# First splits of the first quad and of wo moved into the stage before, A1 loaded in the fold, and ScalarE's order in attention

## The reference

```python
x = x + attn(cond(x, ids1))      # cond: x W1^T + b1 + 2 (x A1[ids1]) B1[ids1]
x = x + ffn(cond2(x, ids2))      # cond2 and ffn: a linear layer each, and experts of rank 16 and 64, top 2

def attn(x):                     # 32 query heads, 8 key/value heads of 128
    q, k, v = x @ wq, x @ wk, x @ wv
    q, k = rope(q), rope(k)
    scores = q k^T * 128 ** -0.5, causal, within a sequence
    return softmax(scores) v @ wo
```

## Time and profile before

| | |
|---|---|
| median of 3 runs | 2829.83 us (2829.41 to 2833.12) |
| profiled execution | 2826.46 us, its span 2824.5 us |
| mean granted clock of TensorE | 0.986 |
| TensorE busy | 2701.7 us, 96% of the span |
| GpSimd busy | 1198.7 us, 42% |
| VectorE busy | 1344.0 us, 48% |
| ScalarE busy | 854.5 us, 30% |
| chain that ended last | TensorE 85%, GpSimd 6%, ScalarE 3%, DMA 2% |

### The profile page before, as it was taken

One profiled execution on the slowest core, in us unless ns is written; L12 is line 12 of the kernel. 1 busy time (PEld: TensorE's weight loads), 2 busy tenths in 40 slices (PEclk: granted clock), 3 DMA queues, 4 the chain that ended last, 5 costly groups with the idle time before them and its releaser, 6 DMA issues.

```text
span 2824.5 us, 37498 instructions
## 1 busy us (share of the span) xinstructions
PE 2701.7 (96%) x14520; PEld 2174.1 (77%) x14520; DVE 1344.0 (48%) x2011; ACT 854.5 (30%) x2089; POOL 1198.7 (42%) x790
## 2 busy tenths in 40 slices
PE   8979899999998999999998989999999899999999
PEld 7857677777776788887877767777777678888877
DVE  2124667777775111124533557777777511112452
ACT  2222244444443312221212224444444331121110
POOL 0025665655665245510304476566555434441020
PEclk9999999999999999999999989999999999999999
DMA  6853122222225333111543312222222433311322
GB/s 217 243 145 119 45 68 73 70 75 68 71 62 189 126 113 105 51 39 54 145 124 100 109 45 76 75 74 63 67 75 72 168 127 112 105 53 38 84 86 70
DMA packets 311984, 268.47 MB, mean 95 GB/s; under 512 B 68218, under 2 KB 283386, under 8 KB 311810
## 3 DMA queue, kind: packets, MB, share of 16 engines
q1 hardware_dynamic: 250210, 210.50, 24.6%
q10 hardware_dynamic: 61600, 55.58, 6.0%
HBM read 201.88 MB, written 64.16 MB: 94 GB/s over the span
## 4 chain that ended last, share of the span: by engine, by line
PE 85%; POOL 6%; ACT 3%; DMA 2%; issue 2%; SPq 1%; DVE 1%; ACTq 0%; POOLq 0%
PE prod L658 25%; PE prod L660 24%; PE prod L659 24%; PE turned L901 3%; PE turned L851 2%; POOL s_lo L1465 2%; POOL o_lo L1499 1%; ACT probs L1227 1%; ACT s_hi L1213 1%; PE turned L652 1%; PE turned L884 1%; PE prod L1086 1%; POOL w_sum L1489 1%; PE prod L766 1%; POOL w_lo L1430 1%
## 5 line engine op out<-in xcount | busy, mean ns | idle before, releaser
L1430 POOL TENSOR_TENSOR w_lo<-raw,w_hi 128x1024 fp32r<-128x1024 f32 x96 | 239.2, 2493 | 850.0 <-ACT w_hi L1146 728.0
L658 PE MATMUL prod<-o_hi,w_hi 128*128 128x512 f32 x1024 | 405.4, 396 | 22.9 <-POOL o_lo L1499 19.2
L659 PE MATMUL prod<-o_lo,w_hi 128*128 128x512 f32 x1024 | 400.8, 391 | 0.0
L660 PE MATMUL prod<-o_hi,w_lo 128*128 128x512 f32 x1024 | 400.4, 391 | 0.0
L1784 DVE TENSOR_TENSOR x<-prod,x 128x512 f32<-128x512 f32 x128 | 88.5, 692 | 603.3 <-PE prod L660 603.3
L1465 POOL TENSOR_TENSOR s_lo<-w_sum,s_hi 128x512 fp32r<-128x512 f32 x192 | 253.0, 1318 | 155.7 <-ACT s_hi L1213 155.7
L658 PE MATMUL prod<-t_hi,s_hi 128*128 128x512 f32 x768 | 312.2, 407 | 3.9 <-POOL s_lo L1465 3.9
L1146 ACT CAST w_hi<-raw 128x1024 fp32r<-128x1024 f32 x128 | 134.1, 1048 | 599.7 <-PE prod L660 428.0
L660 PE MATMUL prod<-t_hi,s_lo 128*128 128x512 f32 x768 | 300.5, 391 | 0.0
L659 PE MATMUL prod<-t_lo,s_hi 128*128 128x512 f32 x768 | 299.8, 390 | 0.0
L658 PE MATMUL prod<-b_hi,s_hi 128*128 128x512 f32 x576 | 239.9, 417 | 15.7 <-POOL s_lo L1465 15.7
(11 more groups left out here) (168 smaller groups left out, 5063.5 us busy)
## 6 DMA issues: line engine op xcount, KB each, us to landing
raw_pair<-in_wq SPq DMA_DIRECT2D x64, 512.0 KB, 4.7
o_scratch<-o_out ACTq DMA_DIRECT2D x64, 512.0 KB, 2.9
raw<-in_wo SPq DMA_DIRECT2D x64, 512.0 KB, 4.0
o_raw<-o_scratch SPq DMA_DIRECT2D x64, 512.0 KB, 7.2
raw<-t_scratch SPq DMA_DIRECT2D x50, 512.0 KB, 3.6
t_scratch<-x ACTq DMA_DIRECT2D x17, 512.0 KB, 4.2
x_raw<-in_x SPq DMA_DIRECT2D x16, 512.0 KB, 5.9
xt_scratch<-x_sum SPq DMA_DIRECT2D x16, 512.0 KB, 3.2
```

Source lines behind the costliest of these rows:

```text
L658: pe.matmul(dst, wh, xh, start=start, stop=False)
L659: pe.matmul(dst, wh, xl, start=False, stop=False)
L660: return pe.matmul(dst, wl, xh, start=False, stop=stop)
L1430: pool.tensor_tensor(WL[i % 2][:], RAW[i % 2][:], WH[i % 2][:].bitcast(F32), ALU.subtract).then_inc(w_lo, 1)
```

## The change

1. `load_a1(0)` moves from the start of stage 1 into the fold loop, ahead of W2's tile 6, into a buffer of its own; `load_a1(1)` moves behind the loads of half 1's first two W1 tiles. ScalarE casts x's blocks 4 to 7 ahead of `AH`, VectorE makes their low parts ahead of `AL`. The cast of W1's tile 2 now stands ahead of the first `c_hi`; for half 1 the first two tiles' casts move within the end of half 0.
2. `load_pair` works in two halves (rows 0 to 511 and 512 to 1023), each with its semaphore. The first half of the next quad is requested after the fourth sum, the second after the sixth low part as before; for the first quad the halves wait for the last two W1 tiles. A k/v pair has now four DMAs instead of two. ScalarE casts the first quad's first two parts ahead of `b22`'s last activation.
3. In attention `turn_p` of the second score block moves from product 0 to product 1 of `QD_KV`, and ScalarE's `p_out` of it likewise, behind the casts `s_high(n + 1, 0)` and `s_high(n + 1, 1)`.
4. ScalarE casts wo's first two tiles at products 2 and 3 of the last quad and the first eight chunks at products 5 and 6. GpSimd makes both tiles' low parts, then chunks 0 to 11; chunks 12 to 15 are VectorE's (`o_lo_d`). The masks of the last group's third and fourth score block stand one product earlier on VectorE, and ScalarE's `exps` of the third.

The diff, cut to its core, in the order SP, TensorE, ScalarE, GpSimd, VectorE (`sp`, `pe`, `act`, `pool`, `dve` in the code):

```diff
-        AW = sb("lora_a_raw", [P, TT * D], offset=88 * KB)
+        AWS = [sb(f"lora_a_raw{hf}", [P, TT * D], offset=o * KB) for hf, o in enumerate((188, 88))]
...
+        def pair_count(n):
+            gg, qd = divmod(n, QUADS)
+            return 16 * (4 * gg + 2 + qd)
...
+        def o_lo_at(hf, kb, i):
+            return (hf * OKB + kb) * 16 - 4 * (hf + (kb > 0)) + i + 1
...
                 if 4 <= i < 8:
                     load_x(0, i - 4)
+                if i == 6:
+                    sp.wait_ge(const_in, 16 * 5)
+                    sp.wait_ge(fold_taken, 4)
+                    load_a1(0)
...
-                if g == 0 and qd == 0:
-                    sp.wait_ge(w_lo, pool_no(hf, T_WO - 1) + 1)
-                else:
-                    sp.wait_ge(s_lo, 7 * (n - 1) + 6)
+                for h in range(2):
+                    ks = slice(4 * h, 4 * h + 4)
+                    if g == 0 and qd == 0:
+                        sp.wait_ge(w_lo, pool_no(hf, T_WO - 2 + h) + 1)
+                    elif h == 0:
+                        sp.wait_ge(s_sum, 4 * (n - 1) + 4)
+                    else:
+                        sp.wait_ge(s_lo, 7 * (n - 1) + 6)
...
-                    sp.wait_ge(tw_turned, TW_N)
-                    load_a1(0)
                     load_x(0, TB - 1)
...
-                        if s == KC - 2:
-                            sp.wait_ge(taken, q_base + Q_O + 4 * 4 + 4)
-                            load_a1(hf + 1)
                 if hf + 1 < HALVES:
                     load_w1(hf + 1, 0)
                     load_w1(hf + 1, 1)
+                    sp.wait_ge(taken, q_base + Q_O + 4 * 4 + 4)
+                    load_a1(hf + 1)
...
-                                if at_ == (QD_KV, 0):
+                                if at_ == (QD_KV, 1):
                                     turn_p(gg - 1, 0, 1)
-                                if at_ == (QD_KV, 1):
                                     score(gg - 1, 1, 0)
...
-                                if j == 0:
-                                    pe.wait_ge(o_lo, (hf * OKB + kb) * 16 + t * KC + k + 1)
+                                if j == 0 and kb == 0 and t == 1 and k >= 4:
+                                    pe.wait_ge(o_lo_d, 4 * hf + k - 3)
+                                elif j == 0:
+                                    pe.wait_ge(o_lo, o_lo_at(hf, kb, t * KC + k))
...
+                for b in range(4, TB):
+                    x_hi(hf, b)
                 act.wait_ge(a_in, 16 * TT * SPT * (hf + 1))
...
-                act.copy(AH[:], AW[:]).then_inc(a_hi, 1)
-                for b in range(4, TB):
-                    x_hi(hf, b)
+                act.copy(AH[:], AWS[hf][:]).then_inc(a_hi, 1)
...
-                for n in range(KC):
+                tile_hi(hf, 2, QN["h0"])
+                c_hi(0)
+                for n in range(1, KC):
                     c_hi(n)
                     tile_hi(hf, n + 2, QN[f"c{n}.0"])
...
+                    if j == 3:
+                        s_high(pair_no(hf, 0, 0), 0)
+                        s_high(pair_no(hf, 0, 0), 1)
...
-                for i in (0, 1, 2, 4, 3, 5, 6):
+                for i in (2, 4, 3, 5, 6):
                     s_high(n0, i)
...
-                                if at_ == (QD_KV, 0):
+                                if at_ == (QD_KV, 1):
                                     p_out(4 * (gg - 1) + 1)
...
+                            if not more:
+                                if i == 2:
+                                    act.wait_ge(qprod, q_done(last, 1))
+                                    tile_hi(hf, T_WO)
+                                if i == 3:
+                                    act.wait_ge(qprod, q_done(last, 3))
+                                    tile_hi(hf, T_WO + 1)
+                                if i in (5, 6):
+                                    for c in range(4 * (i - 5), 4 * (i - 5) + 4):
+                                        o_high(0, c)
...
                 tile_lo(hf, T_WO)
-                for i in range(KC):
-                    o_low(0, i)
                 tile_lo(hf, T_WO + 1)
-                for i in range(KC, 2 * KC):
+                for i in range(KC + 4):
                     o_low(0, i)
...
-                dve.wait_ge(a_hi, hf + 1)
-                dve.tensor_tensor(AL[:], AW[:], AH[:].bitcast(F32), ALU.subtract).then_inc(a_lo, 1)
                 for b in range(4, TB):
                     x_lo(hf, b)
+                dve.wait_ge(a_hi, hf + 1)
+                dve.tensor_tensor(AL[:], AWS[hf][:], AH[:].bitcast(F32), ALU.subtract).then_inc(a_lo, 1)
...
+                for c in range(4, KC):
+                    dve.wait_ge(o_hi, hf * OKB * 16 + KC + c + 1)
+                    dve.tensor_tensor(chunk_of(o_lows(0), c, 1), chunk_of(o_lows(0, OWP), c, 1),
+                                      OH[0][:, c * TOK + NT:(c + 1) * TOK].bitcast(F32), ALU.subtract
+                                      ).then_inc(o_lo_d, 1)
...
+                            if kb == 0 and j == 0 and t == 0:
+                                mask(last_v + 2)
                             if kb == 0 and j == 0 and t == 1:
-                                mask(last_v + 2)
+                                mask(last_v + 3)
                             if kb == 0 and j == 1 and t == 0:
-                                mask(last_v + 3)
                                 normalise(last_v + 2)
```

More of the change, by code:

```diff
@@ L1416, in _ @@
                 if hf + 1 < HALVES:
-                    for i in range(2):
-                        act.wait_ge(raw_in[i], raw_count(hf + 1, i))
-                        act.wait_ge(prod, q_base + Q_O + 4 * (KC - 2 + i) + 2)
-                        act.copy(WH[i][:], RAW[i][:]).then_inc(w_hi, 1)
+                    tile_hi(hf + 1, 1, Q_O + 4 * (KC - 1) + 1 - Q_N)
                 store(KC - 1)
@@ L1471, in _ @@
                         pool.wait_ge(s_lo, 7 * n)
-                    pool.wait_ge(pair_in, 32 * (n + 1))
+                    for h in range(2):
+                        pool.wait_ge(pair_in[h], pair_count(n))
                     if n == pair_no(hf, 0, 0):
```

102 lines of the change are left out of this document (48 added, 54 removed).

## The result

The changed kernel takes 2788.07 us (median, 2785.69 to 2790.83), the kernel before beside it 2830.9: a ratio of 0.9848, 95% interval 0.9831 to 0.9865, 42.8 us faster. The prediction was 2785 us. The profiled execution has a span of 2783.7 us against 2824.5, so 40.8 less; the forecast for it was 44.4 less.

The account below looks back on a forecast made before the run. TensorE, busy 2701.7 of 2824.5 us, was taken to bound the kernel. Terms +9.5 -6.6 -2.9 -21.0 -23.4 = -44.4 take the median from 2829.83 to 2785 us, range 2773 to 2801.

Parts of the forecast that it names:

- Part 1: Fold: A1's half 0 loads on SP ahead of W2's tile 6 delay its products, +9.5 us, ends 8.5 and 12.
- Part 2: Start of half 0: xt_lo wait and c's tile wait go, a new LoRA wait of 4.7 comes; together -6.6 us.
- Part 3: Start of half 1: w_lo waits shrink or go, a new AL wait of 4.7 comes; -2.9 us, ends -9.3 and +2.6.
- Part 4: First quad, both halves: earlier casts and split pair loads shorten GpSimd's chain; -10.5 us each half, -21.0 in all.
- One sign: First quad: the profile after would show the s_lo waits down by over half.
- Part 5: Start of wo, both halves: o_lo starts earlier and VectorE takes four chunks; -11.7 us each half, -23.4 in all.
- Rival (e): Start of wo: o_hi's data or casts hold o_lo to 897.12, only VectorE's four gain; +11.6, 2797 us, chance 0.04.
- Part 6: Steady groups: the 1.35 wait hangs on a chain whose order the diff leaves; 0 us, one end -25.0.
- (a): Steady groups: one more VectorE and GpSimd collision in each of 14 groups, +11.9, 2797.3 us; chance 0.10.
- (b): Steady groups: four ops of each group collide with GpSimd, +66, 2851 us, slower than before; chance 0.03.
- (d): Steady groups: the steady waits go too through GpSimd's earlier start, -25.0, 2760.4 us; chance 0.05.

Follow-up runs that it names:

- the first two experiments on A1: Changed kernel with A1's half 0 loads moved: first, eight behind the fold, eight behind x's blocks 4 to 6, 2776.95 us; second, all ahead of x's block 7, 2776.29 us.
- the third experiment on A1: Changed kernel with A1's half 0 loads in SP's free time, and AH and AL ahead of x's blocks 4 to 7 in both halves: 2766.69 us.
- the last experiment on wo: Changed kernel with ScalarE's casts of wo's first two tiles and first eight chunks behind the last quad's work: 2807.58 us.
- the two swaps: Changed kernel with third block's normalise ahead of fourth's mask on VectorE, 2813.49 us; adding third block's p_out ahead of fourth's exponentials on ScalarE, 2762.35 us.
- the experiment with turn_p and p_out: Changed kernel with turn_p and p_out of the second score block back at product 0 of the k/v quad: 2791.36 us.

## Why the prediction was right, point by point

**Right in sign, size and place.** Every term has the sign that was forecast, and the sum, -44.4, is 3.8 from the profiled -40.6. Two errors are larger than 1 us.

**Part 1 was mis-sized**: +13.0 for +9.5, above its upper end of 12 (its lower end, without the clock, should read 8.7 by its own sum and not 8.5). The wait itself is 9.75 for 8.7, but that it came so near is luck, since the step named there is not the one that TensorE waits for. I had it wait for w_lo, behind a cast and a subtraction; it waits for raw, which the small products of the tile read as it is (L722). The split runs beside them:

```profile
117.99 1.23 DVE L1568 TENSOR_TENSOR w_lo<-raw,w_hi 128x1024 fp32r<-128x1024 f32 x1 [24.50 <-ACT w_hi L1119]
```

```profile
120.43 0.77 PE L672 MATMUL prod<-x_hi,w_hi 128*128 128x512 f32 x1
```

So the 2.4 us of cast, subtraction and hand-offs fall out of the sum. In their place the wait begins 1.7 us ahead of 109.00, where the small products stand, and SP's first A1 issue came at 94.32 and not at 92.4; why SP began 1.9 later is open. The larger miss in the size is the clock: I charged 0.8, and it was 10.2 us at 0.50, 2.9 lost. That the loss is SP's order alone is shown by the first two experiments on A1, that the early load buys nothing by the second of them. The load price, 4.0 by the row, was 4.3 here (issue at 112.58, landed at 116.89). The estimate of 3.2 by the Trainium skill's page DMA: Bandwidth & Descriptors, section Anatomy of one DMA — SWDGE (gpsimd) path, would have been further off.

**Part 2** was -5.7 for -6.6; the lora_a_lo wait is 4.63 for 4.7, w_lo's wait is gone. That wait and two of part 3 belong to a line that the earlier trace rows leaves out, the second of the full list before (8.1 in 3 after):

```profile
PE prod L658 <- POOL w_lo L1430: 19.4, 6, 4.6
```

**Part 3** was -2.9 for -2.9, with the same 4.63. But both parts took A1's place behind x's casts as the price of the gain, and the third experiment on A1 shows that it is none: with the load in SP's free time, AH and AL fit in ahead.

**Part 4** was -11.3 and -11.0 for -10.5 each. The casts ahead of stage 1's end and the split loads are both needed; the loads are worth somewhat more than the 2.8 and 1.0 that I gave them, through the half clock behind v_tok. One sign was missed: the s_lo waits fell by less than half (19.6 to 10.5), since 6.4 of them are left in half 1, and v_tok's wait went nearly whole instead.

**Part 5** was -10.3 and -11.8 for -11.7 each. The start was right (886.14 is 890.65 less the 4.5 gained before; 890.7 forecast). GpSimd's twelve chunks took 17.65 us in place of 15.6, 2.0 more, and I had given back 0.8; four of the six long chunks met VectorE's attention work, which only one of the eight chunks at 1.30 had met, and two met its chunks. Rival (e) did not happen; with the casts behind the last quad, the last experiment on wo starts its chunks at 897.23, 8.8 later against the last group than the changed kernel.

**Part 6** was -0.3 and -0.2 for 0, and the two swaps show the chain, with one correction: it ends at the second wait, and normalise is no link of it. The 1.35 ends with the normalise of the third block, which stands behind a mask and collides with a sum of GpSimd; the 0.44 ends with its copy, which stands behind the fourth block's exponentials on ScalarE. The rule that what the first wait loses the second gains is right for the waits and wrong for the time: the merged stop costs half clock as well. Rivals (a), (b) and (d) did not happen: the waits stayed at 1.35 and 0.43. But the collision of VectorE and GpSimd behind (a) and (b) does stand at a place that TensorE waits for, and did before: the normalise of 1.73 against 0.69 is the one that ends the 1.35. The Trainium skill states the rule behind it in SBUF — State Buffer, section Who interferes with whom. The 1.73 against 0.69 here, and 1.76 against 0.68 in wo, agree with it.

**Open**: what the masks' earlier place (1.43 in each half) and the tile cast ahead of c_hi (3.8) are worth alone, since only the traces show their waits gone and no kernel undid them singly; the 3.3 us of the experiment with turn_p and p_out, and from run to run some 2 us that come and go with the half clock behind the same wait, as at wo of half 1.

## What to carry to other kernels

A load that is moved ahead carries its issues with it: count what they hold up on the issuing queue, and look for a stretch in which that queue is idle before taking one in which it is not. A cast that another engine waits for belongs in front of work that nobody waits for yet, as wo's casts in the last quad and p_out ahead of the exponentials. Two waits that are tied by one chain go together or not at all, and merging them can cost more than both.

## What was not expected of the hardware

One stop of TensorE of 2.17 us is followed by 3.4 us at the 1.2 GHz level in 12 of 14 groups, where stops of 1.35 and 0.43 us, 3.4 us apart, leave the clock at 2.4 GHz: a group with that stretch took 1.7 to 1.8 us longer, a group without it 0.2 or 0.3. A subtraction of 128x512 with both inputs in SBUF takes 1.29 us on GpSimd and 0.68 on VectorE; where the two meet, 1.73 and 1.76. Both engines pay, and means such as 1.47 and 1.43 mix the two kinds.
